# Pre-gate copies, load issues and gate signals of the exact LSTM sweeps put in another place

## The reference

```
x_proj = einsum('btd,gd->btg', x, W_ih) + b_ih + b_hh       # 4 gates x 256 per node
def step((h, c), xp):
    i, f, g, o = split(xp + h @ W_hh.T, 4)
    c = sigmoid(f) * c + sigmoid(i) * tanh(g)
    h = sigmoid(o) * tanh(c)
out = x + 2 * h + prefix sums * fw_att + suffix sums * bw_att   # gated by an argmax of two logits
```

## Time and profile before

| | us |
|---|---|
| median of 3 runs | 2579.7 (2571.73 to 2583.14) |
| the profiled execution | 2585.76 |
| its span, first to last instruction | 2583.9 |
| PE busy, share of the span | 2285.2 (88%) |
| DVE busy | 1720.4 (67%) |
| ACT busy | 1523.0 (59%) |

### The profile page before, as it was taken

The page is one execution under the profiler, slowest core; times in us unless marked ns, Lnnn a source line. Parts: engine busy times, 40 slices in busy tenths (PEclk is TensorE's granted clock), DMA queues, the critical chain, the costliest instruction groups (busy, mean ns, idle before and its releaser), DMA issues.

```text
span 2583.9 us, 46053 instructions
## 1 busy us (share of the span) xinstructions
PE 2285.2 (88%) x14739; PEld 1956.3 (76%) x14739; DVE 1720.4 (67%) x3982; ACT 1523.0 (59%) x2861; POOL 159.2 (6%) x171
## 2 busy tenths in 40 slices
PE   3678989999999999999899999998888888888744
PEld 2467877888888888888787788878887888788723
DVE  5755877777777777777577555555665666566585
ACT  2344447888888888888633444445554555455515
POOL 3233000000000000000000000000000000000060
PEclk7779999999999999999999999999999999999975
DMA  3222320000000000000232112123332333233203
GB/s 95 73 67 76 94 85 22 25 26 26 25 28 24 25 27 29 22 27 24 83 102 67 46 81 87 79 87 109 114 111 81 115 114 111 80 115 114 79 0 99
DMA packets 95190, 174.15 MB, mean 67 GB/s; under 512 B 8983, under 2 KB 69411, under 8 KB 94769
## 3 DMA queue, kind: packets, MB, share of 16 engines
q1 hardware_dynamic: 63378, 86.63, 10.1%
q10 hardware_dynamic: 28108, 81.19, 10.0%
q0 software_dynamic: 3584, 4.76, 0.6%
HBM read 114.14 MB, written 58.36 MB: 67 GB/s over the span
## 4 chain that ended last, share of the span: by engine, by line
PE 59%; DVE 15%; issue 7%; ACT 6%; DMA 2%; ACTq 2%; DVEq 1%; POOL 0%; SPq 0%; POOLq 0%
PE psum L612 23%; PE psum L607 11%; PE psum L762 9%; PE psum L722 8%; DVE scr L1527 3%; DVE scr L1525 2%; ACT scr L1022 2%; PE psum L730 2%; DMA out_dram<-wq 2%; DVE scr L1349 2%; PE psum L718 2%; DVE wp L1445 2%; DVE scr L1523 1%; DVE bufB L1529 1%; ACTq L1033 1%
## 5 line engine op out<-in xcount | busy, mean ns | idle before, releaser
L935 ACT ACTIVATE counts<-psum 125x500 fp32r<-125x500 f32 (+1 forms) x663 | 720.2, 1121 | 160.7 <-PE psum L607 159.1
L612 PE MATMUL psum<-halves,counts 125*125 125x512 f32 x2500 | 743.6, 418 | 2.9 <-ACT counts L935 2.0
L1375 DVE TENSOR_TENSOR wx<-rs_buf 128x500 bf16<-128x500 bf16 (+2 forms) x1326 | 641.4, 530 | 131.8 <-PE psum L607 76.6
L762 PE MATMUL psum<-bufB,wx 128*128 x4800 | 604.1, 283 | 90.1 <-DVE bufB L1529 81.1
L762 PEld LDWEIGHTS psum<-bufB,wx 128*128 128x128 f32 x4800 | 565.4, 194 | 128.6 <-issue 117.8
L612 PEld LDWEIGHTS psum<-halves,counts 125*125 125x125 f32 x2500 | 418.2, 187 | 60.1 <-issue 4.8
L607 PE MATMUL psum<-wx 128*125 128x250 bf16 x2550 | 399.1, 276 | 5.5 <-DVE wx L1375 5.3
L607 PEld LDWEIGHTS psum<-wx 128*125 128x125 bf16 x2550 | 320.6, 138 | 91.3 <-DVE wx L1375 8.6
L722 PE MATMUL psum<-bufA,wx 128*128 (+1 forms) x1600 | 232.6, 289 | 0.0
L722 PEld LDWEIGHTS psum<-bufA,wx 128*128 128x128 f32 x1600 | 194.9, 192 | 23.6 <-issue 0.2
L1022 ACT ACTIVATE scr<-scr 128x125 f32<-128x125 f32 x300 | 92.2, 307 | 168.1 <-DVE scr L1527 168.1
(11 more groups left out here) (262 smaller groups left out, 2418.1 us busy)
## 6 DMA issues: line engine op xcount, KB each, us to landing
bufA<-gates_of_x ACTq DMA_DIRECT2D x144, 500.0 KB, 3.4
gates_of_x<-bufB SPq DMA_DIRECT2D x48, 500.0 KB, 2.6
sums_by_feature<-scr SPq DMA_DIRECT2D x51, 125.0 KB, 2.0
x_times_eps_plus_sums<-rs_buf ACTq DMA_DIRECT2D x10, 625.0 KB
wx<-in_x_dram SPq DMA_DIRECT2D x25, 250.0 KB
x_plus_mix<-wx SPq DMA_DIRECT2D x25, 250.0 KB, 4.9
scr<-x_times_eps_plus_sums SPq DMA_DIRECT2D x50, 125.0 KB
x_times_eps_plus_sums<-scr SPq DMA_DIRECT2D x50, 125.0 KB
```

Source lines behind the costliest of these rows:

```text
L612: return mm(psum[0:TP, 3 + v, :], cnt[v][:, hi, :], xhl[:, hi, :, :].rearrange("p s d -> p (s d)"), start=(hi == 0), stop=(hi == NT - 1))
L762: return mm(half_gates(u, m, slot[0])[:, slot[1], :], whhv[:, k, (2 * gate + m) * P:(2 * gate + m + 1) * P], h, start=False, stop=(k == 1) ...
L935: fn(cnt[v][:, :, 2 * GW * u:2 * GW * u + GW * g].rearrange("p h c -> p c h"), psum[0:TP, u % 3, 0:g * KEYS].rearrange("p (c h) -> p c h", ...
L1375: last = tt(to[:, 0:gs, :, :], tab2[:, 0:k, :].unsqueeze(1).broadcast_to([P, gs, k, 2]), keysT[v][:, part_, g0:g0 + gs, :].unsqueeze(2).br ...
```

## The change

On ACT, the copy of g and o pre-gates (`fill`) is made two steps ahead, into the set of banks that the current step has just finished with. It stands between half 1's sigmoid of o and its tanh of c, behind a wait for that sigmoid's own end (`hso_act`) and one for the load. The load is issued for step t + 3 behind half 0's sigmoid of o. Both sets are filled by ACT before the sweeps begin, and the last two steps of a sweep fill from the kept pre-gates. On PE, g and o have a signal each (`hg_mm`, `ho_mm`), so the tanh of g waits for 18 matmuls of the trace instead of 20 (30 instead of 32 in half 1), the first six matmuls of a step in the program include half 1's g and o instead of its i and f, and PE waits for half 0's sigmoid of o before the last two of half 1. In PSUM the o gate of half m moves to bank 1 - m of the set; for that the first pass keeps the o gate with its two halves swapped, by two copies of 125 columns instead of one of 250. DVE's part of the sweeps is unchanged.

```
+        def gate_half(u, m, g):
+            at, slot = ((2 + m, 0), (2 + m, 1), (m, 0), (1 - m, 1))[g]
+            return psum[:, 4 * u + at, slot * CH:(slot + 1) * CH]
...
-                for g in HALF_ORDER:
+                for g in range(4):
                     half_mm(u, 0, g, 0, h[0])
-                for g in HALF_ORDER[0:2]:
-                    half_mm(u, 1, g, 0, h[0])
+                half_mm(u, 1, 2, 0, h[0])
+                half_mm(u, 1, 3, 0, h[0])
                 pe.wait_ge(S["hh_v"], 2 * done + 2)
                 half_mm(u, 0, 0, 1, h[1])
                 half_mm(u, 0, 1, 1, h[1]).then_inc(S["hif_mm"], 1)
-                half_mm(u, 0, 2, 1, h[1])
-                half_mm(u, 0, 3, 1, h[1]).then_inc(S["hgo_mm"], 1)
-                for g in HALF_ORDER[2:4]:
-                    half_mm(u, 1, g, 0, h[0])
+                half_mm(u, 0, 2, 1, h[1]).then_inc(S["hg_mm"], 1)
+                half_mm(u, 0, 3, 1, h[1]).then_inc(S["ho_mm"], 1)
+                half_mm(u, 1, 0, 0, h[0])
+                half_mm(u, 1, 1, 0, h[0])
                 half_mm(u, 1, 0, 1, h[1])
                 half_mm(u, 1, 1, 1, h[1]).then_inc(S["hif_mm"], 1)
-                half_mm(u, 1, 2, 1, h[1])
-                half_mm(u, 1, 3, 1, h[1]).then_inc(S["hgo_mm"], 1)
+                pe.wait_ge(S["hso_act"], 2 * done + 1)
+                half_mm(u, 1, 2, 1, h[1]).then_inc(S["hg_mm"], 1)
+                half_mm(u, 1, 3, 1, h[1]).then_inc(S["ho_mm"], 1)
...
-                act.wait_ge(S["hgo_mm"], n)
-                fn(tg_c[u][:, 0, m * CH:(m + 1) * CH], half_gates(u, m, 0)[:, 0, :], ACT.Tanh).then_inc(S["htg_act"], 1)
-                fn(s_o[:, m * CH:(m + 1) * CH], half_gates(u, m, 0)[:, 1, :], ACT.Sigmoid)
+                act.wait_ge(S["hg_mm"], n)
+                fn(tg_c[u][:, 0, m * CH:(m + 1) * CH], gate_half(u, m, 2), ACT.Tanh).then_inc(S["htg_act"], 1)
+                act.wait_ge(S["ho_mm"], n)
+                fn(s_o[:, m * CH:(m + 1) * CH], gate_half(u, m, 3), ACT.Sigmoid).then_inc(S["hso_act"], 1)
...
-            def fetch(done, t, u):
-
-                act.wait_ge(S["fill_a"], done + 1)
-                act.wait_ge(S["fill_d"], done + 1)
+            def fetch(filled, t, u):
+
+                act.wait_ge(S["fill_a"], filled)
+                act.wait_ge(S["fill_d"], filled)
                 act.dma_start(pre_in[u].rearrange("p g n -> p (g n)"),
-                              pre_d[ds(t + 2, 1), :, :].rearrange("t p n -> (t p) n")).then_inc(S[f"pre_ld{u}"], 16)
+                              pre_d[ds(t, 1), :, :].rearrange("t p n -> (t p) n")).then_inc(S[f"pre_ld{u}"], 16)
...
+            def sweep_step(done, u, fetched, landed):
+
+                half_gates_out(done, u, 0)
+                if fetched is not None:
+                    fetch(done + 2, fetched, 1 - u)
+                half_cell(done, u, 0)
+                half_gates_out(done, u, 1)
+                act.wait_ge(S["hso_act"], 2 * done + 2)
+                if landed is None:
+                    fill(u, kept[u])
+                else:
+                    act.wait_ge(S[f"pre_ld{u}"], landed)
+                    fill(u, loaded[u])
+                half_cell(done, u, 1)
...
                 with act.Fori(0, LS // 2 - 2) as i:
                     for u in (1, 0):
                         t = 2 * i + 2 - u
-                        done = act.snap(base + t)
-                        fetch(done, t, u)
-                        act.wait_ge(S[f"pre_ld{1 - u}"], 16 * (before + i) + 16)
-                        act.wait_ge(S["hth_act"], 2 * done)
-                        fill(1 - u, loaded[1 - u])
-                        sweep_step(done, u)
...
+                        sweep_step(act.snap(base + t), u, t + 3, before + (16 * i + 32 - 16 * u))
+                sweep_step(act.snap(base + LS - 3), 1, None, before + (8 * LS - 16))
+                sweep_step(act.snap(base + LS - 2), 0, None, None)
+                sweep_step(act.snap(base + LS - 1), 1, None, None)
...
-                    dve.tensor_copy(to[g], psum[:, 4 * u + g, 0:HC]).then_inc(S["kept_v"], 1)
+                    if g == 3:
+                        dve.tensor_copy(to[g][:, CH:HC], psum[:, 4 * u + g, 0:CH])
+                        dve.tensor_copy(to[g][:, 0:CH], psum[:, 4 * u + g, CH:HC]).then_inc(S["kept_v"], 1)
+                    else:
+                        dve.tensor_copy(to[g], psum[:, 4 * u + g, 0:HC]).then_inc(S["kept_v"], 1)
```

More of the change, by code:

```diff
@@ L210, in half @@
             return t[:, :, m * CH:(m + 1) * CH]
-        def half_gates(u, m, pair):
-            return psum[:, 4 * u + 2 * pair + m, 0:HC].rearrange("p (g j) -> p g j", g=2)
+        def gate_half(u, m, g):
+            at, slot = ((2 + m, 0), (2 + m, 1), (m, 0), (1 - m, 1))[g]
+            return psum[:, 4 * u + at, slot * CH:(slot + 1) * CH]
         def fill_to(u, pair):
@@ L236, in build @@
             "sw_d", "sw_v", "cnt_mm", "cnt_z", "flag_v", "w_low", "pre_mm", "kept_v", "pre_st0", "pre_st1", "pre_ld0", "pre_ld1",
-            "hif_mm", "hgo_mm", "hif_act", "htg_act", "hc_v", "hth_act", "hh_v", "fill_a", "fill_d",
+            "hif_mm", "hg_mm", "ho_mm", "hif_act", "htg_act", "hso_act", "hc_v", "hth_act", "hh_v", "fill_a", "fill_d",
             "pe_swept", "lin_v", "lg_mm", "lg_v", "xh_q", "twice_act", "cum_v", "suf_act", "t_v", "out_mm", "out_act", "out_st0", "out_st1", "out_st2", "out_st3")}
@@ L255, in build @@
         GATE_ORDER = (2, 0, 1, 3)
-        HALF_ORDER = (0, 1, 2, 3)
         def skewed(e, iteration, stages):
@@ L760, in half_mm @@
             def half_mm(u, m, gate, k, h):
-                slot = {0: (1, 0), 1: (1, 1), 2: (0, 0), 3: (0, 1)}[gate]
-                return mm(half_gates(u, m, slot[0])[:, slot[1], :], whhv[:, k, (2 * gate + m) * P:(2 * gate + m + 1) * P], h,
+                return mm(gate_half(u, m, gate), whhv[:, k, (2 * gate + m) * P:(2 * gate + m + 1) * P], h,
                           start=False, stop=(k == 1), skip_group_check=True)
@@ L1014, in half_gates_out @@
                 act.wait_ge(S["hif_mm"], n)
-                fn(half(s_if, m), half_gates(u, m, 1), ACT.Sigmoid).then_inc(S["hif_act"], 1)
-                act.wait_ge(S["hgo_mm"], n)
-                fn(tg_c[u][:, 0, m * CH:(m + 1) * CH], half_gates(u, m, 0)[:, 0, :], ACT.Tanh).then_inc(S["htg_act"], 1)
-                fn(s_o[:, m * CH:(m + 1) * CH], half_gates(u, m, 0)[:, 1, :], ACT.Sigmoid)
+                fn(half(s_if, m), psum[:, 4 * u + 2 + m, 0:HC].rearrange("p (g j) -> p g j", g=2), ACT.Sigmoid).then_inc(S["hif_act"], 1)
+                act.wait_ge(S["hg_mm"], n)
+                fn(tg_c[u][:, 0, m * CH:(m + 1) * CH], gate_half(u, m, 2), ACT.Tanh).then_inc(S["htg_act"], 1)
+                act.wait_ge(S["ho_mm"], n)
+                fn(s_o[:, m * CH:(m + 1) * CH], gate_half(u, m, 3), ACT.Sigmoid).then_inc(S["hso_act"], 1)
             def half_cell(done, u, m):
@@ L1022, in half_cell @@
                 fn(th[:, m * CH:(m + 1) * CH], tg_c[1 - u][:, 1, m * CH:(m + 1) * CH], ACT.Tanh).then_inc(S["hth_act"], 1)
[L1024 to L1027, removed]
-            def fetch(done, t, u):
-                act.wait_ge(S["fill_a"], done + 1)
-                act.wait_ge(S["fill_d"], done + 1)
+            def fetch(filled, t, u):
+                act.wait_ge(S["fill_a"], filled)
+                act.wait_ge(S["fill_d"], filled)
                 act.dma_start(pre_in[u].rearrange("p g n -> p (g n)"),
-                              pre_d[ds(t + 2, 1), :, :].rearrange("t p n -> (t p) n")).then_inc(S[f"pre_ld{u}"], 16)
+                              pre_d[ds(t, 1), :, :].rearrange("t p n -> (t p) n")).then_inc(S[f"pre_ld{u}"], 16)
             kept = [[w[:, :, :] for w in pre_kept[v]] for v in range(2)]
             loaded = [[pre_in[v][:, 0:2, :], pre_in[v][:, 2:4, :]] for v in range(2)]
+            def sweep_step(done, u, fetched, landed):
[11 more added lines that the diff above has]
+                half_cell(done, u, 1)
             fill(0, kept[0])
+            fill(1, kept[1])
             k_r_, go = act.alloc_register("act_sweeps"), act.alloc_register("act_go")
@@ L1044, in _ @@
                 base = act.snap(kv * LS)
[L1045 to L1048, removed]
+                before = act.snap(kv * (8 * LS - 16))
+                fetch(base + 1, 2, 0)
+                sweep_step(base, 0, 3, before + 16)
                 with act.Fori(0, LS // 2 - 2) as i:
```

## The result

The changed kernel takes 2571.47 us (median of 20 runs, 2559.56 to 2578.02) where the one before takes 2580.54 (20 runs, 2571.73 to 2588.07): 9.1 us less. The ratio is 0.9965, with a 95% interval of 0.9954 to 0.9976. That is clear of no change, less than 0.5%, and more than twice what was forecast. A ratio here goes by all fast runs, so it can differ a little from the quotient of the two medians. The profiled execution took 2574.78 us, its span 2572.9.

What follows compares the result with a forecast made beforehand. It took a ring of waits through both halves to bound the sweeps: 144 steps x (0.14 - 0.09) = 7.2 us less, 3.2 more in the first pass, net 4.0 less than 2579.7, so 2576 us; range 2562 to 2591.

Steps and rivals of the forecast that it cites:

- rival A: Copy in half 1 hides, 0.02 us or less late; 17 to 20 us less, 3.2 more: 2563 to 2566; chance 0.22.
- The ring: Sweep steps: waits through h, PE, ACT and DVE in both halves, not a full engine, set the 4.54 us step.
- the early tanh of g: Half 0: g and o signalled apart start tanh of g earlier, L1525 0.14 us earlier per step; bounds 0 and 0.16.
- The copy off the first sigmoid: Odd steps: pre-gate copy no longer before L1015; overlaps with the early g signal, so both step kinds gain the same 0.14.
- The copy in its new place: Half 1, between sigmoid of o and tanh of c: makes tanh of c 0.09 us late; bounds 0 and 0.24.
- The load's issue: L1033, behind half 0's sigmoid of o: hidden before tanh of c with 0.07 us to spare; bounds 0 and 0.17.
- Rival C: ACT's queue bounds both halves: 0.26 us late against 0.14 gained per step, plus 3.2 us: 2600; chance 0.14.
- PE's new wait: Second half's last two gates wait for half 0's sigmoid of o: costs 0, with 0.28 us to spare.
- The first pass: Low-precision pass before the sweeps: split copy of gate 3 costs 0.065 us a step, 3.2 us; bounds 0 and 7.
- The sum: Whole kernel: 7.2 us less in the sweeps, 3.2 more in the pass, net 4.0 less, 2576 us.

Runs made afterwards that it cites:

- e4: Changed kernel, but the tanh of g waits for o's signal again; ratio 1.0062 to the kernel before, 2596.14 us.
- e3: Changed kernel with load issue and pre-gate copy back at the head of a step; signals, banks, PE order, split copy kept; ratio 0.9944, 2568.11 us.
- e2: Changed kernel with ACT's wait for the load put before its wait for the sigmoid's end, ahead of the copy; ratio 0.9940, 2565.67 us.
- e1: Kernel before, with only the first pass's copy of gate 3 split in two of 125 columns; ratio 1.0014, 2584.76 us.

## Why the prediction was right, and where a size was off

The measured 2571.47 us lie in the stated range of 2562 to 2591, but that range is 29 us wide and also holds the unchanged kernel's 2580 and rival A's times, and 2571.47 is about as near to A (2563 to 2566) as to the forecast (2576). What bears the mechanism out are the distances in the traces and the experiments. One of the signs named beforehand missed: the step was to be 4.48 to 4.50 and is 4.45.

**The ring, and the early tanh of g.** Right. L1524 of half 0 was foretold 0.61 behind its sigmoid in both kinds of step, and is 0.62 and 0.63. The forecast gain was 0.14, and that came (tanh of c 1.26 instead of 1.41 in the step shown, 0.143 by the medians over a sweep), limited by DVE's spacing as said. e4 shows that the gain needs this signal: without it the change costs 0.62%.

**The copy off the first sigmoid.** Right that it doesn't add up with the signal. What wasn't drawn from it is that the copy's old place costs little once the signals are apart: e3 keeps it there, and the copy makes the first sigmoid 0.09 late in every second step only (0.02 of it is made up by the closer L1530), less on average than the new place costs in every step.

**The copy in its new place.** The mechanism was right, the size was not, and this is the term that halved the forecast. It was put at 0.09 late, by a register step of 0.10 as L1054 has it, and came to 0.06 a step. The instructions of the register step, in the changed kernel:

```profile
L1046 ACTq FUSED_REGOPS  x141: 43/68/91, 1753.5 to 2420.6; - x141
```

Inside a sweep it takes 0.068 us in one kind of step and 0.086 in the other. The copy so started 0.14 and 0.16 behind the sigmoid's end (0.12 to 0.18 had been foretold), and the tanh of c came 0.07 and 0.08 later than in the kernel before. That is half of the miss. The other half is a link that the forecast held constant: behind the copy the tanh of c is 0.29 long instead of 0.31, and h ends 0.72 instead of 0.74 after its start, so 0.02 comes back. Per step the gain is 0.087 instead of 0.05: 12.5 us and not 7.2. The lateness stayed within what the rows had given (0.04 to 0.10). Rival A, a copy that hides, holds in e2 and not in the change: 2565.67 us, in A's 2563 to 2566.

**The load's issue.** Hidden, as forecast, with more to spare: it ends at 1912.80, 0.20 before the tanh of c, since the steps in front of the DMA itself took 0.28 from the sigmoid of o (1912.18 to 1912.46) and not 0.36. Rival C, in which it overran, did not come. No run took its cover away, so what it costs uncovered was not tried.

**PE's new wait.** Not seen to hold: the 29th matmul of a step starts 1.88 us behind the 13th in the trace of before and in that of after. The 0.28 to spare were worked out; no run used them up. In the changed trace the sigmoid ends at 1912.46, with 0.13 to a matmul 1912.59, and the 29th matmul starts at 1912.85, which leaves 0.26.

**The first pass.** 3.2 us forecast, 3.1 measured, alone (e1) and in the change. The two copies are 0.20 apart and 0.28 long, as the nearest rows of other operations had it. The Trainium skill's fixed cost per instruction ("VectorE: DVE Perf Modes", "The TRN2 errata") had 0.125 a step and 6.3 us; the trace has 0.06 to 0.07, so the measurement decides against that reading of it: the second copy starts 0.20 after the first, which is 0.29 long, so part of what each costs lies beneath the other.

**The sum.** Forecast 4.0 less, measured 9.1. The 5.1 between them are what the copy's term and the shorter link behind it gave, 12.5 - 7.2 = 5.3, the rest being less than the measurement tells.

## What to carry to other kernels

In a ring of short operations look at which instruction of a group carries the signal: two matmuls that the tanh of g did not need were 0.14 us of every step, more than a move of the whole copy could bring. A wait for an engine's own last operation put 0.09 us before the next one here, which the ring did not feel; with a register value computed behind it it was 0.14 to 0.16, which it did. So put first the wait whose value must be computed. An edit made for the layout of another stage, here one copy turned into two, costs where that stage waits for the last of them; put it at another place in the order.

## What was not expected of the hardware

The first interval of a sweep starts after the test between two sweeps, in which PE is busy for 0.20 of 7.13 us (1971.27 to 1978.40). Part of the interval runs at 1.2 GHz and part at 2.4, and how much differs from sweep to sweep with the same work: the interval takes 6.57 and 5.57 us in the second and third sweep of the changed kernel.

```profile
1978.40:1984.97 6.57, 6.57 (x33) 6.57 (x34) 1.16 (x4) 1.50 (x5) 0.00 (x0) 0.54 0.35 108
2210.12:2215.69 5.57, 5.28 (x32) 5.09 (x33) 1.22 (x5) 1.50 (x7) 0.00 (x0) 0.72 0.39 112
```

The granted clock is 0.54 and 0.72 of full there, between the two levels; the shorter interval has the higher one. One microsecond per sweep is as much as many an edit of this kernel is worth, so the length of a step is better read from intervals well inside a sweep.
